# The middle stage's first tokens, keys, queries and values made in the first stage's last batch

## The reference, cut to what matters

```python
x = x + tanh(g_xattn[0]) * L0_xattn(layernorm(x), ctx)      # 16 heads of 16
x = x + tanh(g_ffn[0])   * L0_ffn(layernorm(x))             # 8 experts, top 2
x = x + tanh(g_xattn[1]) * L1_xattn(ctx, layernorm(x))      # 16 heads of 64, keys = [LN(ctx), LN(x)]
x = x + tanh(g_ffn[1])   * L1_ffn(layernorm(x))             # 8 experts, top 2
```

## Time and profile before

| what | value |
|---|---|
| runs | 1386.5, 1386.49, 1382.69 us; median 1386.49 |
| profiled execution | 1383.62 us, its span 1381.8 us |
| busy share of the span | TensorE 88%, VectorE 78%, ScalarE 72%, GpSimd 59% |
| granted TensorE clock, mean | 0.947 of full speed |
| weight loads on TensorE | 63% |

### The profile page before, as it was taken

How to read it: one execution, slowest core, us unless ns; L and a number is a source line. 1 busy time by engine, 2 the same in 40 slices (tenths; PEclk the granted TensorE clock), 3 DMA queues, 4 the chain that set the end, 5 groups by cost and what they waited for, 6 DMA issues and landing times. The chain is left out here.

```text
span 1381.8 us, 38075 instructions
## 1 busy us (share of the span) xinstructions
PE 1221.0 (88%) x13060; PEld 875.3 (63%) x13060; DVE 1075.3 (78%) x3112; ACT 996.3 (72%) x2552; POOL 812.9 (59%) x1204
## 2 busy tenths in 40 slices
PE   5899999999986499999999999999999986299994
PEld 3777777777764245666566666565666555299984
DVE  4899999999995168888888888888888875377772
ACT  4888888888883358887878887878877873166662
POOL 3544555445432346677777777777777765255654
PEclk8899999999997599999999999999999996599998
DMA  6545455445320148877788777888768797833323
GB/s 185 153 137 162 138 146 167 125 122 157 98 63 7 49 94 159 138 146 139 161 163 155 142 149 145 153 164 149 145 143 154 145 196 184 340 63 64 57 36 76
DMA packets 309406, 185.50 MB, mean 134 GB/s; under 512 B 257930, under 2 KB 295186, under 8 KB 306112
## 3 DMA queue, kind: packets, MB, share of 16 engines
q1 hardware_dynamic: 292448, 134.26, 46.3%
q0 software_dynamic: 13168, 35.80, 10.5%
q10 hardware_dynamic: 3600, 13.02, 2.8%
HBM read 76.19 MB, written 49.94 MB: 91 GB/s over the span
## 5 line engine op out<-in xcount | busy, mean ns | idle before, releaser
L1707 ACT ACTIVATE b_prob<-b_prob,b_top 112x487 f32<-112x487 f32 x256 | 178.9, 699 | 28.0 <-DVE b_top L1844 26.2
L1340 POOL TENSOR_TENSOR w_pool<-b_prob,w_pool 112x487 f16<-112x487 f32 x128 | 146.8, 1147 | 82.7 <-ACT w_pool L1732 81.3
L1518 PE MATMUL b_ps_p<-w_s,b_tok_s 128*128 128x512 f16 (+1 forms) x768 | 187.7, 381 | 4.0 <-DVE w_pool L1831 3.2
L1518 PE MATMUL b_ps_p<-b_tok_s,w_s 128*128 128x487 f16 x768 | 183.1, 376 | 6.4 <-POOL b_tok_s L1334 3.7
L1844 DVE CUSTOM_DVE_ANT_0 b_prob<-b_ps_s,b_keep 112x487 f32<-112x487 f32 x256 | 167.3, 654 | 14.7 <-PE b_ps_s L1611 13.1
L739 ACT ACTIVATE w_pool<-w_pool,a_top 112x375 f32<-112x375 f32 x256 | 155.0, 605 | 5.3 <-DVE a_top L874 2.2
L1732 ACT ACTIVATE w_pool<-b_prob 112x487 f16<-112x487 f32 x256 | 155.9, 609 | 0.4
L874 DVE CUSTOM_DVE_ANT_0 w_pool<-a_ps_s,a_keep 112x375 f32<-112x375 f32 x256 | 137.6, 537 | 14.9 <-PE a_ps_s L632 14.6
L640 PE MATMUL a_ps_t<-a_const,w_pool 112*125 112x112 f32 x768 | 134.2, 284 | 12.7 <-ACT w_pool L739 10.3
L1626 PEld LDWEIGHTS b_ps_o<-w_pool 128*128 128x128 f16 (+1 forms) x3072 | 124.5, 100 | 30.7 <-DMA w_pool<-w_pool 11.1
L879 DVE TENSOR_TENSOR w_pool<-a_ps_t,w_pool 125x336 f16<-125x336 f32 x256 | 127.7, 499 | 20.7 <-ACT w_pool L746 19.7
(11 more groups left out here) (261 smaller groups left out, 2963.6 us busy)
## 6 DMA issues: line engine op xcount, KB each, us to landing
xs<-w_pool SPq DMA_DIRECT2D x14, 1032.0 KB, 4.2
...
```

The source lines that it names most:

```text
L1340: pool.tensor_tensor(halves[:, h % TURN, LO, 0:NK], prob[:, h % RING, 0:NK], halves[:, h % TURN, HI, 0:NK], ALU.subtract).then_inc(s_lo[1], 1)
L1518: last = pe.matmul(out, sta(a, k), mov(m, k), start=(k == 0 and n == 0), stop=(k == tiles - 1 and n == 2))
L1707: act.activation(prob[:, h % RING, 0:NK], prob[:, h % RING, 0:NK], ACT.Exp, bias=top[:, h % RING:h % RING + 1], scale=-1.0, accum_out=sums ...
```

## The change

The front of stage two is taken out and its work is put into stage one's program. A class `Ahead` holds the buffers and semaphores that both stages now share (const, affine, tokens, statistics, `tok_s`, `q_s0`, and keys and values in `w_pool`); in stage one's division of `w_pool` next_f comes first and the float32 weights last, so that batch 0's keys and values lie on next_f, which is free by then. Four small memsets and the loads of g1, b1, g2, b2 move to stage one too.

- Batch 14: SP loads affine values and the tokens of batch 0 at the head of its body; VectorE takes their statistics in slot 13.
- Batch 15: GpSimd makes the deviation, ScalarE normalises in slot 2, TensorE turns in slots 3, 4, 5, ScalarE evicts in slots 4, 5, 6, GpSimd splits; then the same for batch 1 (loads behind s_norm, statistics in slot 8, normalisation in slot 13), whose turns come in the end of the stage.
- End of stage one: the 18 products of batch 0 and the three turns of batch 1 stand between the transposes, values and ditems of the serial end; the last ten products follow the last ditem.
- Stage two begins with its loop. What is left ahead of it: masks, four loads, the router's split, constants, second bias, first chunks.

The bodies of the new functions are those of stage two (L1302, L1814, L1710, L1718, L1522), with the buffers of `nxt`; the diff is cut to their waits and to the places where they are called.

```diff
+        NSLOTS = (3, 4, 5)
+
+        def next_bank(k):
+            return ps_t[0] if ITEMS[k][0] == "q" else ps_s[sum(kind != "q" for kind, _ in ITEMS[:k]) % 2]
...
+            def next_tokens(c):
+
+                if c == 0:
+                    for n, v in enumerate(nxt.affine_in):
+                        sp.dma_start(nxt.affine[:, n, :], v).then_inc(nxt.s_setup, 16)
+                    sp.wait_ge(s_store, 16 * 2)
+                else:
+                    sp.wait_ge(nxt.s_norm, 2)
+                sp.dma_start(nxt.ctx_t[:, :, :], nxt.ctx_tok[c].rearrange("(j p) d -> p j d", p=KB0)).then_inc(nxt.s_cload, 16)
+                sp.dma_start(nxt.x2_t[:, :], x2_dram[c]).then_inc(nxt.s_xload, 16)
+
             def body(b, par):
+                if b == B - 2:
+                    next_tokens(0)
...
                 if not ahead(b, 1):
+                    next_tokens(1)
                     load_residual(b)
...
+            def next_deviation(c):
+
+                pool.wait_ge(nxt.s_stats, 8 * c + 8)
...
+            def next_split(c, k):
+
+                cols = TOK[k]
+                pool.wait_ge(nxt.s_thi, NI1 * c + k + 1)
+                pool.tensor_tensor(nxt.tok_s[c][(slice(None), LO) + cols], nxt.tok_f[(slice(None),) + cols],
+                                   nxt.tok_s[c][(slice(None), HI) + cols], ALU.subtract).then_inc(nxt.s_tsplit, 2)
+
             def body(b, par):
+                if not ahead(b, 1):
+                    next_deviation(0)
...
+                if not ahead(b, 1):
+                    for k in range(NI1):
+                        next_split(0, k)
+                    next_deviation(1)
...
+            def next_turn(c, k):
+
+                if c == 0:
+                    ps = ps_p[k]
+                    if k == 0:
+                        pe.wait_ge(s_ifree, PI * B)
+                        pe.wait_ge(s_dfree, DI * (B - 2))
+                else:
+                    ps = ps_t[1]
+                    if k == 0:
+                        pe.wait_ge(s_plo, H * B)
+                    else:
+                        pe.wait_ge(nxt.s_nfree, NI1 + k)
+                if k == 0:
+                    pe.wait_ge(nxt.s_norm, 2 * c + 2)
+                if k < KT:
+                    for j in range(NB0):
+                        last = pe.transpose(ps[:, j * KB0:(j + 1) * KB0], nxt.ctx_n[:, j, k * 128:(k + 1) * 128], ident[0:KB0, 0:KB0])
...
+            def next_item(k):
+
+                ps = next_bank(k)
+                kind, n = ITEMS[k]
+                if k == 0:
+                    pe.wait_ge(nxt.s_tsplit, 6)
+                    pe.wait_ge(s_nhi, H)
+                    pe.wait_ge(s_nlo, H)
+                    pe.wait_ge(s_max, H * B)
+                if kind == "q":
+                    pe.wait_ge(s_plo, H * B)
+                    if n:
+                        pe.wait_ge(nxt.s_ifree, ITEMS.index(("q", 0)) + 1)
+                elif before_bank(k) > 0:
+                    pe.wait_ge(nxt.s_ifree, before_bank(k))
+                tok = nxt.tok_s[0]
+                if kind == "k":
+                    last = product(ps[:, 0:NK], lambda a, d: next_kv[:, a, d, n * 128:(n + 1) * 128], lambda a, d: tok[:, a, d, 0:NK])
...
+                    if not ahead(b, 1) and s in NSLOTS:
+                        next_turn(0, NSLOTS.index(s))
...
-            drain(B - 1, 1)
-            for k in range(DI):
+            transposes(B - 1, H - 2)
+            values(B - 1, 1, H - 4)
+            next_item(0)
+            transposes(B - 1, H - 1)
+            values(B - 1, 1, H - 3)
+            next_item(1)
+            values(B - 1, 1, H - 2)
+            values(B - 1, 1, H - 1)
+            next_turn(1, 0)
+            next_item(2)
+            next_turn(1, 1)
+            next_item(3)
+            next_turn(1, 2)
+            next_item(4)
+            ditem(B - 1, D_XT)
+            next_item(5)
+            ditem(B - 1, D_GATE)
+            next_item(6)
+            ditem(B - 1, D_PAIRS[0])
+            ditem(B - 1, D_PAIRS[1])
+            next_item(7)
+            for k in range(D_CWT, DI):
                 ditem(B - 1, k)
+            for k in range(8, PI1):
+                next_item(k)
...
+            def next_normalise(c):
+
+                act.wait_ge(nxt.s_rstd, 3 * c + 3)
+                if c:
+                    act.wait_ge(nxt.s_nitem, NI1 * c)
...
+            def next_turned(c, k):
+
+                ps = ps_t[1] if c else ps_p[k]
+                act.wait_ge(nxt.s_nitem, NI1 * c + k + 1)
+                if k == 0:
+                    act.wait_ge(nxt.s_setup, 16 * 4)
+                    if c:
+                        act.wait_ge(nxt.s_tsplit, 6 * c)
+                if k < KT:
+                    act.activation(nxt.tok_f[:, k, 0:C], ps[:, 0:C], ACT.Identity, bias=nxt.affine[:, 1, k:k + 1], scale=nxt.affine[:, 0, k:k + 1]).then_inc(nxt.s_nfree, 1)
...
+                act.wait_ge(nxt.s_nfree, NI1 * c + k + 1)
+                act.activation(nxt.tok_s[c][(slice(None), HI) + cols], nxt.tok_f[(slice(None),) + cols], ACT.Copy).then_inc(nxt.s_thi, 1)
...
+                    if not ahead(b, 1):
+                        if s == 2:
+                            next_normalise(0)
+                        if s - 1 in NSLOTS:
+                            next_turned(0, NSLOTS.index(s - 1))
+                        if s == 13:
+                            next_normalise(1)
...
             phi(B - 1, H - 2)
+            next_item(0)
             phi(B - 1, H - 1)
+            next_item(1)
             out_lo(B - 1)
+            next_turned(1, 0)
+            next_item(2)
+            next_turned(1, 1)
+            next_item(3)
+            next_turned(1, 2)
+            next_item(4)
             ditem(B - 1, D_XT)
+            next_item(5)
             weigh(B - 1)
-            for k in range(D_PAIRS[0], DI):
+            next_item(6)
+            ditem(B - 1, D_PAIRS[0])
+            ditem(B - 1, D_PAIRS[1])
+            next_item(7)
+            for k in range(D_CWT, DI):
                 ditem(B - 1, k)
+            for k in range(8, PI1):
+                next_item(k)
...
+            def next_stats(c):
+
+                dve.wait_ge(nxt.s_cload, 16 * c + 16)
+                for j in range(NB0):
+                    dve.bn_stats(nxt.bns[0:KB0, j, :], nxt.ctx_t[:, j, :]).then_inc(nxt.s_stats, 1)
+                dve.wait_ge(nxt.s_xload, 16 * c + 16)
+                dve.bn_stats(nxt.bns[0:T, NB0, :], nxt.x2_t[:, :]).then_inc(nxt.s_stats, 1)
+                dve.wait_ge(nxt.s_zero, 4)
+                if c:
+                    dve.wait_ge(nxt.s_rstd, 3 * c)
+                dve.wait_ge(nxt.s_stats, 8 * c + 4)
+                for j in range(NB0):
+                    dve.bn_aggr(nxt.mv[0:KB0, j, :], nxt.bns[0:KB0, j, :]).then_inc(nxt.s_stats, 1)
...
+                    if b == B - 2 and s == 13:
+                        next_stats(0)
+                    if b == B - 1 and s == 8:
+                        next_stats(1)
...
             plo(B - 1, H - 2)
+            next_item(0)
             plo(B - 1, H - 1)
+            next_item(1)
             read_out(B - 1, 1)
+            next_item(2)
+            next_item(3)
             stats_x1(B - 1)
+            next_item(4)
             norm_x1(B - 1)
             ditem(B - 1, D_XT)
+            next_item(5)
             ditem(B - 1, D_GATE)
             rank_experts(B - 1)
             combine_weights(B - 1)
-            for k in range(D_PAIRS[0], DI):
+            next_item(6)
+            ditem(B - 1, D_PAIRS[0])
+            ditem(B - 1, D_PAIRS[1])
+            next_item(7)
+            for k in range(D_CWT, DI):
                 ditem(B - 1, k)
+            for k in range(8, PI1):
+                next_item(k)
...
-                load_tokens(c)
...
             pool.wait_ge(s_zero, 8)
-            deviation(0)
             mask_bias(0, 0)
-            for k in range(NI):
-                split_tokens(0, 0, k)
-            deviation(1)
-            for k in range(NI):
-                split_tokens(1, 1, k)
-            pool.wait_ge(s_setup, 16 * 9)
+            pool.wait_ge(s_setup, 16 * 8)
             pool.tensor_copy(wr_s[:, HI, :, :], wr_f[:, :, :]).then_inc(s_wsplit, 1)
...
+                if first(b) and h == 0:
+                    pe.wait_ge(s_zero, 8)
...
-            pe.wait_ge(s_setup, 16 * 9)
-            pe.wait_ge(s_zero, 8)
-            for c, items in ((0, range(4)), (1, range(4, PI))):
-                for k in range(NI):
-                    need(pe, s_nfree, NI, c, k)
-                    nitem(c, k)
-                for k in items:
-                    if ITEMS[k][0] == "q":
-                        pe.wait_ge(s_nfree, 2 * NI)
-                        pe.wait_ge(s_ifree, ITEMS.index(("q", 0)) + ITEMS[k][1])
-                    item(0, 0, k)
-            pe.wait_ge(s_wsplit, 2)
             run_batches(pe, body)
...
-            act.dma_start(const[:, :], consts).then_inc(s_setup, 16)
```

(26 more changed lines are left out.)

247 lines of the change are left out of this document (176 added, 71 removed).

## The result

The changed kernel takes 1382.53 us (median of 12 runs, 1380.25 to 1384.86), the kernel before 1385.19 in 12 runs beside it: ratio 0.998, 95% interval 0.9971 to 0.9988. That is a gain of 2.7 us, small but clear of the noise, where 12 were forecast.

What follows compares the result with a forecast made beforehand. At the handover between stages no engine runs at its own pace; TensorE bounds stage two behind that. -53.05 + 2 + 7 + 18.3 + 1.5 + 12.3 = -11.95 from 1383.6 gives 1371.7, forecast 1372 us, range 1360 to 1384.

Steps and rivals of the forecast that it cites:

- case (d): Stage one pays all: batch 14 at 4, batch 15 at 10, drain's clock 4, new wait 14; 1380.9 us; chance 0.12.
- Part 1: Front of stage two, from its first transfer to its first scores, is removed: -53.05 us.
- near 478: Sign in the changed profile: the first scores of stage two start near 478 us.
- Part 2: Batch 14 of stage one: added load issues and VectorE's token statistics cost +2 us, 0 to 4.
- part 3: Batch 15 of stage one: ScalarE's two normalisations and evictions, with VectorE's statistics, cost +7 us, 2 to 10.
- part 4: End of stage one: products between the serial steps cost +18.3 us, and a slow clock start +1.5, 0 to 8.
- idle over 5 us in the drain: Sign against the forecast: if TensorE idles this long at stage one's end, part 4 is wrong.
- Rival (c): TensorE's clock stays at half through stage one's drain; 1392.7 us; chance 0.08.
- Part 5: Start of stage two: VectorE's maxima of head 5 wait for GpSimd's low half behind its setup; +12.3 us, 8 to 16.
- Rival (a): Start of stage two: VectorE is not held at head 5, the wait is only 3.5 us; 1362.9 us; chance 0.2.
- Rival (b): Start of stage two: TensorE restarts at half clock, 2.5 products at 1.0 us more; 1374.2 us; chance 0.15.
- what is saved stays saved: Behind its start, TensorE bounds stage two, so the saving was taken to last; no later loss was charged.

Runs made afterwards that it cites:

- experiment 1: Changed kernel with batch 14's affine and first-token loads issued behind the mask and residual instead of ahead; 1376.26 us, ratio 0.993 to the kernel before.
- experiment 2: Changed kernel with only the four affine loads issued a batch earlier, at the end of batch 13; 1382.19 us in one run.
- experiment 6: On top of experiment 4, the second tokens' statistics and normalisation moved from batch 15 into the drain; 1367.74 us, ratio 0.9854 to the kernel before.
- experiment 7: On top of experiment 3, first tokens loaded at the end of batch 13 and normalised in batch 14; 1371.35 us, ratio 0.989 to the kernel before.
- experiment 3: Changed kernel with GpSimd's set-up of stage two spread over that stage's batch 0; 1377.17 us, ratio 0.9948 to the kernel before.
- experiment 4: Changed kernel with the edits of experiment 1 and experiment 3 together; 1370.32 us, ratio 0.9902 to the kernel before.
- Experiment 9: The kernel before, unchanged, run again for a second trace; 1385.57 us.

## Why the prediction was wrong, point by point

**The range and the likeliest case.** 1372 was forecast, 1382.5 came, near the upper end of the range (1360 to 1384); case (d), stage one pays all, forecast 1380.9, is nearest in number and right on batch 15 (10), but it has at most 4 for batch 14 and puts the rest on the drain's clock and the wait, which came as forecast. The removed front and the new wait came as forecast; one term of the sum was far too small, and two losses, the restart and the end, stood outside it.

**Part 1**, the front of 53.05 us, is gone: the first scores start at 482.97, 0.2 us after the stage ("near 478" was forecast; batches 14 and 15 took 8.4 us more than forecast, the drain 2.9 less).

**Part 2, batch 14, is the step that failed**: +7.3 where +2, at most 4, was charged. I saw both halves, the 2.7 us of issuing and the tokens "ahead of it in the same queue", and even that GpSimd already waits for this residual. Then I charged 1 us, counting on later work to cover the rest. Later work covers only a third of it: GpSimd's next step would have waited 2.2 us for VectorE anyway (experiment 1). The other 4.1 us go on over x1 and its statistics on VectorE to the turn on TensorE, each of them behind other work in an engine's queue, and TensorE stands 4.19. The clock falls behind that stop and adds 2.6 us, for which the sum had nothing in batch 14. The second miss is that the transfer ahead was given no number, though the tokens' landing could have been read from the earlier trace rows (issue 449.04, use 455.36). Experiment 1 removes 6.6 us of the 7.3 by swapping the issues, experiment 2 parts issuing from transfers.

**Parts 3 and 4** were +26.8 together and came out +27.0, which is luck: the errors cancel. Batch 15 took 10.1 instead of 7, the drain 16.9 instead of 19.8 (18.3 and 1.5 for the clock). The two normalisations, named in part 3, are at work: experiments 6 and 7 take one of them out each and win 2.6 and 3.4 us of batch 15. The other part is the clock, for which the sum had only the 1.5 in part 4. TensorE is at half clock for more than half of batch 15:

```profile
416.00:434.00 18.00, 14.72 (x95) 11.73 (x95) 12.67 (x44) 11.67 (x33) 6.27 (x12) 0.50 0.12 36
```

Over the whole batch it is busy 26.51 us for 193 instructions, where it was busy 19.90 for 185. How much of the 10.1 us is the clock alone no run parts; the second trace of the kernel before has 0.79 and 24.2 us where the first has 0.93 and 23.1. The drain's walk was 1.4 too long and its 1.5 for the clock was not needed, but it was not tested against its alternative: the interleaving is worth only 5.8 us. One of the prediction's own signs is met: "idle over 5 us in the drain". TensorE is idle 5.8 of the 39.4 us, 3.34 of them before x1's turn, where 1.7 was expected, and 1.65 behind the last product, where the stages change. Rival (c), a clock at half through the drain, is refuted: 0.96 granted.

**Part 5, the new wait**, is right in place, releaser and size (+12.9 for +12.3), and experiment 3 removes 7.3 of the 12.9 us. Rival (a) is refuted.

**Rival (b), the restart at half clock**, came beside the forecast: the product behind the wait takes 2.62, the clock of the stretch is 0.83, and the rest of batch 0 is 1.8 us longer; (b) said 2.5. The Trainium skill (TensorE: Matmul & The Clock Gate, Part 1: The HAM clock gate) says that throttled is the default; the 2.62 behind the stop agrees. The restart should have been in the sum and not among the rivals, since the forecast itself had TensorE stand still. That it makes up all of the 1.8 us is not shown: TensorE also waits 2.24 us for a transfer at 513.10, and the rest of batch 0 is still 28.7 and 29.6 us in experiments 3 and 4, where the stop is shorter and GpSimd has its set-up to do in that batch.

**The end**, +3.3 from the last maxima of stage two on, was in nobody's account: "what is saved stays saved" was argued from stage two alone. Experiment 9 makes mere spread unlikely (the least difference of any two traces is 2.3); the cause is open.

Of the 10.5 us between the forecast and the trace, 5.3 are batch 14, 3.3 the end, 1.8 the rest of batch 0, 0.6 the wait and 0.2 parts 3 and 4; 0.7 come back elsewhere.
